# Reload of the node sums: the fourth tile's load moved behind the last tile's load

## The chip, the cores and the metric

The kernel runs on one core of a Trainium2 chip. The metric is the device time of one execution in microseconds (us), the median over several runs; lower is better. A core has a matrix engine (TensorE, "PE" in the profile), a vector engine (VectorE, "DVE"), a scalar engine (ScalarE, "ACT"), a general engine (GpSimd, "POOL") and an engine that issues most of the transfers (SyncE, "SP"). SP, ACT and POOL each have a DMA queue; in the profile SP's is q1, ACT's is q10 and POOL's is q0. All of them are served by the same 16 DMA engines. Engines wait for one another on semaphores.

## The reference, cut to what matters

A graph layer over 625 nodes with 512 features each and 10625 edges: a tensor-product message per edge, summed by target node; a linear-attention mixing of the nodes; and a feed-forward stage with two shared experts and 64 routed ones, of which each node takes six.

```python
xn = layernorm(x)
x1 = xn[src].reshape(-1, 16, 32); x2 = edge_attr.reshape(-1, 16, 32)
contrib = coeffs[None, :, None] * x1[:, i1, :] * x2[:, i2, :]      # 64 paths
edge_out = zeros.at[:, i3, :].add(contrib)
gnn = zeros.at[dst].add(edge_out)                                   # sum over edges by node
x = x + gnn + linear_attention(xn)
x = x + moe(layernorm(x))                                           # 2 shared, 64 routed, top 6
```

## The kernel before, in words

The edges are sorted by target node. The nodes are cut into ten windows of 64 (`NW = 10`, `W = 64`), numbered w = 0 to 9; the last window holds nodes 576 to 624. A window is worked in four chunks of 16 paths (`CHUNKS = 4`), so there are 40 chunks k. For a chunk DVE multiplies the gathered node rows with the edge rows (L1202, one instruction per path), and PE sums the products by target node with one-hot matrices (L1667; L1675 for the last window) into PSUM banks.

When a window's four chunks are summed, ACT copies the two banks to a staging buffer and stores them to `sums_d` in DRAM (`flush`, L870 to L874): two DMAs of 64 rows of 4 KB, 512 KB in all, each counted by `s_stored[w % 2]`. This is done for windows 0 to 8. The ninth window (w = 8) is the last one stored in this way, and the change speaks of it as the ninth group. The tenth window isn't stored: its sums are added from PSUM by DVE (`add_last`, L1296).

The sums come back in another tiling. The array `sums` has five tiles t = 0 to 4 of 125 nodes, with a row of 2048 numbers (8 KB) for each node, and lies in the SBUF tensor `arena`. Each tile is loaded by two DMAs, rows 0 to 111 and rows 112 to 124 (`PARTS`), except the last tile (nodes 500 to 624). Of that only the 76 rows of nodes 500 to 575 come from DRAM, by DMAs of 64 and 12 rows; the rest has been cleared by ACT (L879, `s_zeroed`). Tile 3 is nodes 375 to 499 and so needs windows up to w = 7 only (nodes 448 to 511); tile 4 needs the ninth window, w = 8 (nodes 512 to 575).

SP's program at this place (L522 to L532), in its order: wait until DVE has finished the products of window 8 (`s_prod`), wait until windows 0 to 7 are stored, load tiles 0 to 3 (eight DMAs, L528), wait until ACT has cleared the rest of tile 4, wait until window 8 is stored (`s_stored[0]`), load tile 4's rows (two DMAs, L532). Each of the ten DMAs adds 16 to `s_sums`. After them SP waits for the last chunk on PE (`s_chunk`) and then issues the loads of the feed-forward weights (L565, L554, L557, L568, L560), the first ones without a wait between them.

DVE, when it has made the last products, waits for all ten loads at once (`dve.wait_ge(s_sums, 16 * 10)`, in `sum_and_normalize`), adds the tenth window (L1296) and sums the 64 paths into the node features (`path_sum`, L1288); then come the layer norm (L1314 to L1330), the transposes on PE (L1764), the router and the experts. A branch for edges that the fixed windows don't hold (`missed`) isn't taken with these inputs.

Of the kernel before, what the change touches and what calls it, by code (L numbers as in the profile page):

```python
# [22 lines left out]
TT, TR, DC = 5, 125, 4  # L23
HALVES = ((0, 313), (313, 312))
PARTS = ((0, 112), (112, TR))
# [13 lines left out]
LATE = (NW - 1) * W - (TT - 1) * TR  # L39
TOP = 64  # L40
# [129 lines left out]
def gps_layer(nc, x, src, dst, edge, coeffs, paths, wqkv, rm, wout, bout,  # L170
              wr, swg, swu, swd, wg, wu, wd, out):
    with ExitStack() as ctx:
# [5 lines left out]
        def sem(name):  # L178
            return ctx.enter_context(nc.semaphore(name))
# [13 lines left out]
        prod, x1, x2, stage, sums, pair = m["prod"], m["x1"], m["x2"], m["stage"], m["sums"], m["pair"]  # L193
# [146 lines left out]
        s_sums = sem("s_sums")  # L340
# [8 lines left out]
        onehot, rtab, rank, selb, parts, cnt_row, extra = (m[k] for k in ("onehot", "rtab", "rank", "selb", "parts",  # L349
                                                                         "cnt_row", "extra"))  # L350
# [125 lines left out]
        def _(sp):  # L476
# [45 lines left out]
            sums_tiles = sums_d[0:N, :].rearrange("(t p) c -> p t c", t=TT)  # L522
            sp.wait_ge(s_prod, CHUNKS * (NW - 1))
            for b in range(2):
                sp.wait_ge(s_stored[b], 32 * (NW // 2 - 1))
            for t in range(TT - 1):
                for a, b in PARTS:
                    sp.dma_start(sums[a:b, t, :], sums_tiles[a:b, t, :]).then_inc(s_sums, 16)  # L528
            sp.wait_ge(s_zeroed, 1)
            sp.wait_ge(s_stored[0], 32 * (NW // 2))  # L530
            for a, b in ((0, TOP), (TOP, LATE)):
                sp.dma_start(sums[a:b, TT - 1, :], sums_tiles[a:b, TT - 1, :]).then_inc(s_sums, 16)  # L532

            sp.wait_ge(s_cover, 1)
            missed = sp.value_load(more_v[:, :], min_val=0, max_val=1)
# [1450 lines left out]
```

## Time and profile before

| | us |
|---|---|
| median of 3 runs | 1015.66 |
| lowest and highest run | 1013.46, 1018.88 |
| the profiled execution, its own time | 1019.58 |
| the profiled execution, span from first to last instruction | 1017.5 |
| PE busy | 895.9 (88% of the span) |
| DVE busy | 548.1 (54%) |
| ACT busy, POOL busy | 256.0 (25%), 268.2 (26%) |
| data moved by DMA | 300.68 MB, mean 296 GB/s |
| mean granted TensorE clock | 0.961 |

The span falls into an edge stage (to about 321 us), the sum over the paths with the layer norm and the router (to about 396 us), and the experts. Times in the profile are counted from the first instruction. A DMA that an engine issues shows as a short row at its issue; its packets run later on the DMA engines. The view of the DMA queues counts, for a stretch of time, each queue's packets that started in it, their megabytes, and the time that they took as a share of the time of 16 engines. A packet of a tile reload is a row of 8 KB, one of a store of window sums 4 KB. Each DMA engine that takes part in a DMA closes it with a packet of 4 bytes, the completion; it counts as "under 512 B". The view counts a DMA of 112 rows with its completions as 128 packets, one of 13 rows as 26.

### The profile page before, as it was taken

To read this page: it belongs to the slowest core of one execution; us is meant where nothing else is said; L and a number is where in the kernel's file an instruction comes from. 1 tells how busy PE (TensorE), PEld (TensorE's weight loads), DVE (VectorE), ACT (ScalarE), POOL (GpSimd) and SP (SyncE) were. 2 spreads that over 40 slices of the span, in tenths; PEclk is the share of its full clock that TensorE was granted. 3 is DMA by queue.
4 is the path that set the end of the run, shared out by engine and by line. 5 is a ranking of instruction groups with operands and counts; after the bars stand their busy time and mean duration, and the time that the engine had idled before them with its cause. 6 is when DMAs were issued, how large, how long until landed. Compare 5 with 4: busy or idle time off the path is not lost. (4 is left out here: it accounts for less than half of the span.)

```text
span 1017.5 us, 20833 instructions
## 1 busy us (share of the span) xinstructions
PE 895.9 (88%) x7497; PEld 589.3 (58%) x7497; DVE 548.1 (54%) x1623; ACT 256.0 (25%) x573; POOL 268.2 (26%) x265
## 2 busy tenths in 40 slices
PE   1599998897878298999999999999999989999991
PEld 1355555564544196676556566766676765656660
DVE  7997987978798986323324333334233332333216
ACT  2111101121130132333322322333233322322331
POOL 4543321334300102222222222222222322222211
PEclk9699999999989789999999999999999999999996
DMA  8856454565428951889979999999988999999976
GB/s 276 287 207 207 158 186 171 207 207 208 166 63 279 373 206 57 319 303 367 405 290 334 359 383 413 390 387 361 405 307 332 353 400 398 365 374 366 402 289 262
DMA packets 76929, 300.68 MB, mean 296 GB/s; under 512 B 13730, under 2 KB 14119, under 8 KB 58548
## 3 DMA queue, kind: packets, MB, share of 16 engines
q1 hardware_dynamic: 57256, 254.21, 65.9%
q0 software_dynamic: 17280, 38.48, 10.5%
q10 hardware_dynamic: 2252, 6.06, 1.7%
q8 instruction: 95, 1.56, 0.6%
q14 instruction: 46, 0.38, 0.1%
HBM read 290.26 MB, written 26.62 MB: 311 GB/s over the span
## 5 line engine op out<-in xcount | busy, mean ns | idle before, releaser
L1202 DVE TENSOR_TENSOR arena<-arena 128x288 f32 (+1 forms) x640 | 236.3, 449 | 37.8 <-remote 24.5
L1826 PE MATMUL bank<-arena,low 128*64 128x256 f32 x2048 | 241.6, 383 | 2.0 <-issue 2.0
L1667 PE MATMUL bank<-arena,multi 128*64 128x256 f32 x1296 | 162.0, 400 | 44.0 <-DVE arena L1202 32.6
L1826 PEld LDWEIGHTS bank<-arena,low 128*64 128x64 f32 x2048 | 141.0, 137 | 75.6 <-issue 12.4
L1851 PE MATMUL bank<-arena,low 128*64 128x256 f32 x1392 | 161.6, 379 | 1.1 <-ACT low L980 1.1
L1667 PEld LDWEIGHTS bank<-arena,multi 128*64 128x64 f32 x1296 | 99.5, 144 | 102.2 <-issue 44.2
L743 POOL DMA_INDIRECT low<-xr_d,idx x64 | 90.2, 1409 | 238.7 <-DVE place L1433 177.6
L747 POOL DMA_INDIRECT y_d<-low,place x64 | 68.5, 1070 | 262.3 <-ACT low L987 181.8
L1851 PEld LDWEIGHTS bank<-arena,low 128*64 128x64 f32 x1392 | 101.3, 137 | 50.3 <-ACT low L980 1.3
L987 ACT ACTIVATE low<-bank,gcol 64x256 f32<-64x256 f32 x174 | 82.1, 472 | 105.0 <-PE bank L1851 103.9
L687 POOL DMA_INDIRECT arena<-xn_d,ssel x79 | 90.3, 1143 | 38.2 <-issue 21.8
L1438 DVE TENSOR_TENSOR low<-low,bank 128x256 f32<-128x256 f32 x64 | 39.2, 613 | 103.4 <-ACT low L983 102.8
L1492 DVE TENSOR_TENSOR low<-low,bank 64x512 f32<-64x512 f32 x23 | 24.7, 1075 | 101.9 <-ACT low L1023 80.7
L1791 PE MATMUL bank<-xT_,arena 128*128 128x208 f32 (+1 forms) x384 | 74.8, 349 | 5.1 <-ACT low L970 2.6
L983 ACT ACTIVATE low<-bank 128x256 f32<-128x256 f32 x64 | 24.7, 386 | 207.1 <-PE bank L1826 207.1
L1791 PEld LDWEIGHTS bank<-xT_,arena 128*128 128x128 f32 x384 | 67.9, 192 | 11.9 <-issue 8.9
L1836 PE MATMUL bank<-arena,low 128*32 128x256 f32 x928 | 55.5, 381 | 0.2 <-issue 0.2
L1417 DVE TENSOR_TENSOR low<-iota,multi 125x640 bf16<-125x640 f32 x64 | 52.2, 816 | 0.0
L977 ACT COPY low<-bank 128x512 f32<-128x512 f32 x64 | 37.6, 587 | 37.8 <-PE bank L1815 35.5
L1836 PEld LDWEIGHTS bank<-arena,low 128*32 128x32 f32 x928 | 27.9, 110 | 25.5 <-issue 9.5
L1815 PE MATMUL bank<-ident,low 128*128 128x128 f32 x256 | 40.7, 281 | 2.2 <-DMA low<-xr_d,idx 1.7
L1815 PEld LDWEIGHTS bank<-ident,low 128*128 128x128 f32 x256 | 28.9, 140 | 22.0 <-issue 19.5
(214 smaller groups left out, 710.9 us busy)
## 6 DMA issues: line engine op xcount, KB each, us to landing
arena<-in_L_ffn_Wg_dram SPq DMA_DIRECT2D x64, 1024.0 KB
arena<-in_L_ffn_Wu_dram SPq DMA_DIRECT2D x64, 1024.0 KB
arena<-in_L_ffn_Wd_dram SPq DMA_DIRECT2D x64, 1024.0 KB
arena<-in_edge_attr_dram SPq DMA_DIRECT2D x88, 256.0 KB
arena<-y_d SPq DMA_DIRECT2D x5, 1250.0 KB, 6.8
sums_d<-arena ACTq DMA_DIRECT2D x18, 256.0 KB, 3.2
arena<-sums_d SPq DMA_DIRECT2D x4, 896.0 KB
arena<-in_L_mix_W_qkv_dram SPq DMA_DIRECT2D x2, 1024.0 KB, 18.1
```

The lines of the kernel that those rows point to most:

```text
L687: pool.indirect_dma_start(x1[b][:, i, :], None, xn_d, bass.IndirectOffsetOnAxis(ap=ssel[:, at + i:at + i + 1], axis=0)).then_inc(s_x1[b], 16)
L743: return pool.indirect_dma_start(xg[:, to, :], None, xr_d, bass.IndirectOffsetOnAxis(ap=idx[:, i:i + 1], axis=0), bounds_check=N - 1, oob_ ...
L747: return pool.indirect_dma_start(y_d, bass.IndirectOffsetOnAxis(ap=place[:, i:i + 1], axis=0), yy[:, b, :], None, bounds_check=Y_ROWS - 1, ...
L987: ins = act.activation(yy[64 * o:64 * o + 64, b, h * HF:(h + 1) * HF], out_bank[64 * h:64 * h + 64, 0:HF], ACT.Copy, scale=gcol[64 * h:64 ...
L1202: return dve.tensor_tensor(prod[:, buf, 0:n, EXT * p:EXT * p + EXT], x1[b][:, 0:n, bass.ds(i1, EXT)], x2[b][:, 0:n, bass.ds(i2, EXT)], ALU ...
L1417: return dve.tensor_tensor(onehot[0:TR, b], iota[0:TR, None, bass.ds(base, CAP2)].to_broadcast([TR, TT, CAP2]), ranks[:, :, None].to_broad ...
L1667: ins = pe.matmul(bank[2 * b + c // 2][64 * h:64 * h + 64, 256 * (c % 2):256 * (c % 2) + 256], pair[:, pairs, i, :], prod[:, buf, i, 256 * ...
L1791: ins = pe.matmul(shared_bank(u)[:, 256 * w:256 * w + nn], shgu[:, w, k, c * 128:(c + 1) * 128], xT[:, k, a:a + nn], start=(w == 0 and k = ...
L1815: ins = pe.transpose(bank[1][:, c * 128:(c + 1) * 128], xg[:, b, c * 128:(c + 1) * 128], ident[:, :])
L1826: ins = pe.matmul(out_bank[64 * h:64 * h + 64, w * HF:(w + 1) * HF], xgT[:, b, k, 64 * o:64 * o + 64], gu[:, slot, w, k, h * HF:(h + 1) * HF],
L1836: ins = pe.matmul(out_bank[at:at + PART, q * HF:(q + 1) * HF], xgT[:, b, k, CAP + PART * q:CAP + PART * (q + 1)], gu[:, slot, w, k, h * HF ...
L1851: ins = pe.matmul(out_bank[64 * h:64 * h + 64, 0:HF], lhs, dn[:, slot, k, h * HF:(h + 1) * HF], start=(k == 0), stop=(k == DC - 1), skip_g ...
```

## The change

SP loads only tiles 0, 1 and 2 at once. The two waits (on the clearing and on the store of window 8) come next, then the load of tile 4's rows, and after it the load of tile 3. No transfer is added or dropped, the sizes are the same, and DVE still waits for all ten. The loop has become a helper `reload`, so all of these DMAs are recorded under L528; lines below the place have four added to their number.

```diff
-            for t in range(TT - 1):
-                for a, b in PARTS:
+            def reload(t, parts):
+                for a, b in parts:
                     sp.dma_start(sums[a:b, t, :], sums_tiles[a:b, t, :]).then_inc(s_sums, 16)
+
+            reload(0, PARTS)
+            reload(1, PARTS)
+            reload(2, PARTS)
             sp.wait_ge(s_zeroed, 1)
             sp.wait_ge(s_stored[0], 32 * (NW // 2))
-            for a, b in ((0, TOP), (TOP, LATE)):
-                sp.dma_start(sums[a:b, TT - 1, :], sums_tiles[a:b, TT - 1, :]).then_inc(s_sums, 16)
+            reload(TT - 1, ((0, TOP), (TOP, LATE)))
+            reload(3, PARTS)
```

SP's row before, from the last edge load to the next wait; the 112- and 13-row loads are tiles 0 to 3, the 64- and 12-row loads tile 4:

```order
L495 DMA arena<-in_edge_attr_dram 128x512
L528 DMA arena<-sums_d 112x2048 [waits s_stored1,s_stored0,s_prod]
L528 DMA arena<-sums_d 13x2048
L528 DMA arena<-sums_d 112x2048
L528 DMA arena<-sums_d 13x2048
L528 DMA arena<-sums_d 112x2048
L528 DMA arena<-sums_d 13x2048
L528 DMA arena<-sums_d 112x2048
L528 DMA arena<-sums_d 13x2048
L532 DMA arena<-sums_d 64x2048 [waits s_stored0,s_zeroed]
L532 DMA arena<-sums_d 12x2048
L535 TENSOR_LOAD more_v [waits s_cover]
```

The same piece of SP's row in the changed kernel:

```order
L495 DMA arena<-in_edge_attr_dram 128x512
L528 DMA arena<-sums_d 112x2048 [waits s_stored1,s_stored0,s_prod]
L528 DMA arena<-sums_d 13x2048
L528 DMA arena<-sums_d 112x2048
L528 DMA arena<-sums_d 13x2048
L528 DMA arena<-sums_d 112x2048
L528 DMA arena<-sums_d 13x2048
L528 DMA arena<-sums_d 64x2048 [waits s_stored0,s_zeroed]
L528 DMA arena<-sums_d 12x2048
L528 DMA arena<-sums_d 112x2048
L528 DMA arena<-sums_d 13x2048
L539 TENSOR_LOAD more_v [waits s_cover]
```

The fourth pair of 112 and 13 rows has moved past the wait and past the 64 and 12 rows; six loads stand ahead of the wait in place of eight. No other engine's row changes, apart from line numbers.

## Rows read from the trace of the kernel before

**Rows 1.** Waits on PE, from 358 us to the end: total, times, longest.
```profile
PE bank L1791 <- ACT low L970: 2.6, 1, 2.6
```
**Rows 2.** Busy time in stretches: PE, PEld, DVE, ACT, POOL, clock, DMA share, GB/s.
```profile
357.60:361.50 3.90, 3.86 (x17) 3.16 (x18) 3.87 (x6) 1.81 (x4) 0.00 (x0) 0.50 1.01 426
361.50:366.20 4.70, 4.70 (x44) 4.70 (x44) 3.87 (x4) 2.38 (x3) 0.00 (x0) 0.99 1.01 360
...
396.00:1012.00 616.00, 592.37 (x5485) 388.06 (x5485) 214.79 (x703) 181.47 (x406) 155.47 (x126) 0.99 0.92 354
```
**Rows 3.** Waits of SP's queue, 290 to 325 us.
```profile
SPq L528 <- DVE arena L1202: 17.4, 1, 17.4
SPq L530 <- DMA sums_d<-arena: 14.1, 1, 14.1
```
**Rows 4.** Timeline, 285 to 375 us: start, duration, what, idle before it.
```profile
297.49 3.57 SPq L528 DMA_DIRECT2D arena<-sums_d  x8
...
300.40 17.20 DVE L1202 TENSOR_TENSOR arena<-arena 128x224 f32 x56
...
302.77 1.10 ACTq L874 DMA_DIRECT2D sums_d<-arena  x2
...
315.22 1.07 SPq L532 DMA_DIRECT2D arena<-sums_d  x2
...
321.33 0.85 DVE L1296 TENSOR_TENSOR arena<-arena,bank 61x256 f32<-61x256 f32 x2 [3.73 <-DMA arena<-sums_d]
...
324.45 6.87 SPq L560 DMA_DIRECT2D arena<-in_L_ffn_Wd_dram  x2
...
357.64 4.42 PE L1764 MATMUL bank<-ident,low 125*128 125x125 f32 x20 [19.38 <-DVE low L1330]
```
**Rows 5.** DMA queues, 297.4 to 302.7 us: packets, MB, share of 16 engines.
```profile
q1 hardware_dynamic: 151, 1.07, 80.2%
```
**Rows 6.** DMA queues, 302.7 to 308.9 us, the stretch behind the store's issue.
```profile
DMA packets 194, 1.30 MB, mean 210 GB/s; under 512 B 35, under 2 KB 35, under 8 KB 35
q1 hardware_dynamic: 194, 1.30, 97.3%
```
**Rows 7.** DMA queues, 308.9 to 311.1 us.
```profile
q1 hardware_dynamic: 67, 0.52, 61.0%
q10 hardware_dynamic: 66, 0.26, 37.3%
```
**Rows 8.** DMA queues, 311.1 to 312.1 us.
```profile
q10 hardware_dynamic: 45, 0.13, 64.2%
q1 hardware_dynamic: 37, 0.17, 49.0%
```
**Rows 9.** DMA queues, 312.1 to 314.3 us.
```profile
q1 hardware_dynamic: 80, 0.56, 76.4%
q10 hardware_dynamic: 49, 0.13, 23.9%
```
**Rows 10.** DMA queues, 314.3 to 316.3 us; no packet of q10.
```profile
q1 hardware_dynamic: 72, 0.43, 85.4%
```
**Rows 11.** DMA queues, 316.3 to 321 us.
```profile
DMA packets 120, 0.67 MB, mean 143 GB/s; under 512 B 38, under 2 KB 38, under 8 KB 38
q1 hardware_dynamic: 119, 0.66, 62.4%
```
**Rows 12.** Timeline, ACT, 60 to 300 us: two other stores of window sums.
```profile
186.64 1.10 ACTq L874 DMA_DIRECT2D sums_d<-arena  x2
...
276.39 1.10 ACTq L874 DMA_DIRECT2D sums_d<-arena  x2
```
**Rows 13.** DMA queues, 277.45 to 279.75 us; no packet of q10 from 276.39 to 277.45.
```profile
q10 hardware_dynamic: 160, 0.52, 84.9%
```
**Rows 14.** DMA queues, 186.64 to 189.3 us; q10's 160 packets follow by 191.6.
```profile
q0 software_dynamic: 212, 0.70, 69.4%
q1 hardware_dynamic: 192, 0.33, 34.1%
```

## The prediction

> **What bounds the kernel now.** I read the whole from the end. Behind 358 us PE hardly waits: its longest wait after the router begins is 2.6 us [rows 1], and over the 616 us of the experts it is busy 592.37 us [rows 2]. What arrives late at the start of that stretch therefore comes late at the end, nearly one for one. The start is set by DVE: PE sat idle 19.38 us before L1764, until DVE had finished the layer norm [rows 4], and DVE works without a gap worth naming from L1296 at 321.33 us. What released L1296 is the place of the change: DVE made its last product by 317.60 us (300.40 + 17.20) and idled 3.73 us for the loads from `sums_d` [rows 4]. So these loads are on the path that sets the end, and 3.73 us is also the most that any order of them could bring, 0.37% of the time.
>
> Next, what makes the loads late. SP's own waits [rows 3]: 14.1 us for the store of the ninth group, before tile 4's load. That looks like the thing to shorten. But the DMA view of the same stretch shows that the wait costs little: q1 carries the reloads all along. Its packets up to 321 us are 151, 194, 67, 37, 80, 72 and 119 [rows 5 to 11], together 720. Four tiles make 4 x (128 + 26) = 616, tile 4's part (64 rows with 16 completions, 12 with 12) makes 104: 720 again, so nothing is missing from the count. By 316.3 us 601 had started, 15 short of tile 3's end; tile 4's load was issued at 315.22 and needs about one more microsecond to its first packet. Tile 4 joined the end of tile 3 almost without a hole. The loads are bound by the pace of their queue, not by the wait.
>
> **What the change does to the sum.** It removes and adds nothing: the same ten loads, 4.72 MB, on the same queue, the same wait on DVE. It takes 154 of the 720 packets (tile 3, 1.02 MB) out of the part that is queued before the wait and puts them behind it. So the question is whether q1 still has work while SP waits.
>
> 1. Tiles 0 to 2 are 3 x 154 = 462 packets. By 312.1 us 449 of q1's packets had started (151 + 194 + 67 + 37, [rows 5 to 8]). In the new kernel q1 runs dry soon after 312.1.
>
> 2. When does the store land? It was issued at 302.77 [rows 4]; up to 308.9 there is no packet of q10 at all [rows 6]; then the two queues take turns, 66 against 67 packets [rows 7]. By 312.1, 111 of its 160 packets had started; the other 49 took until 314.3 beside tile 3 [rows 8, 9]. Nothing in the first 6 us changes if the cause is the load already in progress, so I keep the start at 308.9. Only the last 49 packets lose their competitor. Alone, 160 packets took 2.3 us [rows 13], so 49 would take 0.7 and end at 312.8; if the slowest engine is still busy with tile 2 they end as before, 314.3. I take 313.4.
>
> 3. From the landing to SP's issue: 314.3 to 315.22 is 0.9 us. From an issue to the first packet in a quiet stretch: 276.39 to 277.45, 1.05 us [rows 12, 13]. First packet of tile 4 at 313.4 + 0.9 + 1.05 = 315.35. Between some 312.5 and 315.35 q1 moves nothing, where before it moved tile 3.
>
> 4. Then 201 rows, 1.65 MB. Before, the last 271 packets of q1, likewise 1.65 MB, ran from 312.1 to 321, 8.9 us with the tail of the slowest engine [rows 9 to 11]. At the pace of a full queue, 210 GB/s [rows 6], they would take 7.8 us. I take 8.4: last packet at 323.75, and DVE starts 0.3 us later, as before (321.0 to 321.33): 324.05.
>
> The wait ends 2.7 us later than 321.33. The bounds: landing at 312.8 and tile 0's pace (1.07 MB in 5.3 us less the first 1.05 [rows 5], 252 GB/s, so 6.5 us) give 321.55, +0.2 us. Landing at 314.3, tile 4 at 210 GB/s (3.0 us) and tile 3 at the 143 GB/s of the last stretch [rows 11] (7.2 us) give 326.75, +5.4 us.
>
> **What is queued behind the longer wait.** On SP, after the two moved loads, come the wait for the last chunk and the weight loads. They were issued from 320.94, behind a wait for PE; the moved loads are issued by about 316.4, so SP isn't late, but the first weights now stand behind tile 3 on the same queue. PE starts again only at 357.64 [rows 4], and with transposes that need no weights, so that lateness of a few us is covered by more than 30. ACT and PE wait for nothing that moves. PE's idle time before L1764 grows from 19.38 to about 22 us. After that gap the granted clock is 0.50 up to 361.5 and 0.99 behind it [rows 2], the 1.2 and the 2.4 GHz level; a later start can shift that edge as well. I cost it at nothing in the forecast and at half of a 3.9 us stretch, 2 us, in the slow rival.
>
> Against its own profiled execution the sum is 1019.58 + 2.7 = 1022.3. The profiled execution is 3.9 us above the median of the runs, so the forecast for a median is 1015.66 + 2.7 = 1018.4.
>
> **A rule of the skill beside it.** Rows 6 and 7 show 6.1 us without a packet of the store and equal turns behind it. The Trainium skill, page "DMA: Bandwidth & Descriptors", section "Queues, rings and completion order", says that each DMA engine goes round between the queues that have work, a packet at a time. By the rule alone the store would take its turns from about 303.8 in both kernels, and the rule doesn't explain the 6.1 us. Where the store shared the engines the trace agrees with it; where it stood still, it does not. If the start of the store came from the queue ahead of it, it could move with the change, and that is the first rival.
>
> **Rivals.** *The store starts earlier.* With six loads ahead of it in place of eight, it might begin one tile sooner: at 308.9 two tiles were through (345 packets had started, two tiles are 308, [rows 5, 6]); should the chip let a store in when only two queued tiles are left, that point is one tile sooner now. If it begins near 304.5 and takes the 5.4 us that it took beside the loads, it lands at 309.9, SP issues at 310.8, the first packet comes at 311.85, before q1 is dry. Then there is no hole, the same 720 packets run at the same pace, and the wait ends as before: 0 us, 1015.7. For it: a store issued at 276.39, with no work on q1, started after 1.05 us, and one at 186.64, with 192 packets of q1 ahead, only after 2.7 [rows 12 to 14]; work on q1 does hold a store back. Against it: SP could put seven larger loads and more into the queue before it was held, at 324.45 for 6.87 us [rows 4], so eight reloads are not beyond what the queue takes, and the store passed tiles 2 and 3, so it didn't wait for all that was issued before it.
>
> *The mixture is faster.* Beside the store q1 moved 0.52 MB in 2.2 us, 236 GB/s, against 210 alone [rows 6, 7]. If the store starts early and the whole queue holds that pace, 4.72 MB take 20.0 us from 298.5, and DVE starts at 318.8: 2.5 us sooner, 1013.2. Against it: in the other shared stretch q1 moved only 0.17 MB in 1.0 us [rows 8].
>
> *Slower.* The store lands no sooner than before and tile 3, now last, meets the slow end of the queue, where 0.67 MB took 4.7 us [rows 11]: the upper bound above, +5.4 us, 1021.1; with the clock's edge moved as well, up to 1023. This decides if the store's last packets are held by the slowest engine's tile 2 and not by tile 3.
>
> **How the numbers follow.** Forecast (+2.7 us, 0 to +4): 0.50. The store starts earlier (0 us): 0.25. Faster mixture (-2.5 us): 0.08. Slower (+5.4 to +7.4 us): 0.17. Half a percent is 5.1 us, about what a measurement of this kernel tells from no change (its three runs lie 5.4 us apart). Faster by more than that is beyond the 3.73 us that DVE idles, so it needs the spread of the runs: 0.04. Slower by more: most of the slow rival and a little of the forecast's spread: 0.12. Within: 0.84. The range takes in the faster mixture in part and the upper bound, with some 1.5 us for the spread of a median: 1013.2 to 1022.5.
>
> **What would show it.** In the new profile: SP's wait for the store shorter by about 1 us and not by 4 or 5; a stretch of 2 to 3 us around 313 to 315 us in which q1 moves nothing; tile 4's issue near 314.3; weight loads still issued at 321; DVE idle before L1300 (L1296 before) about 6.4 us in place of 3.73; everything behind it later by the same amount. The prediction is wrong if the store's first packet comes before 307, if q1 has no hole, or if DVE's idle time stays near 3.7 us.

## The result, and the profile after

The changed kernel takes 1020.64 us (median of 20 runs), the kernel before 1016.73 us (20 runs). The ratio of their runs is 1.0043, with a 95% interval of 1.0027 to 1.0059: slower by 4.4 us, between 2.7 and 6.0 (the two medians are 3.9 us apart). The forecast was +2.7 us, at the lower edge of that interval; 1020.64 lies in the forecast's range, 1013.2 to 1022.5.

The profiled execution of the changed kernel spans 1020.0 us against 1017.5. Its first reload is issued 4.1 us earlier than before (293.40 against 297.49), which is the spread of the edge stage, so I compare stretches and not points of time. The timeline of the changed kernel, same columns as [rows 4]; the ten loads are now one merged row because they share a line:

```profile
293.40 18.94 SPq L528 DMA_DIRECT2D arena<-sums_d  x10
...
298.69 1.10 ACTq L878 DMA_DIRECT2D sums_d<-arena  x2
...
316.97 0.37 SPq L569 DMA_DIRECT2D arena<-in_L_ffn_sWg_dram  x1
...
321.01 0.85 DVE L1300 TENSOR_TENSOR arena<-arena,bank 61x256 f32<-61x256 f32 x2 [7.37 <-DMA arena<-sums_d]
...
357.45 4.30 PE L1768 MATMUL bank<-ident,low 125*128 125x125 f32 x20 [23.16 <-DVE low L1334]
```

DVE now idles 7.37 us for the loads in place of 3.73 [rows 4], 3.64 us more. From the first reload's issue to DVE's add it is 27.61 us against 23.84, from that add to PE's transposes 36.44 against 36.31. PE's idle time in front of the transposes grew by 3.78 us. The 3.7 us arise at the reload, and the stage from the add to the transposes passes them on whole. How much of them reaches the end only the runs tell: in single profiles the time from the transposes to the end of the span scatters more than that, 659.9 us before, 662.6 in the changed kernel, and 657.6 in e4 below.

SP's wait for the store, changed kernel, against 14.1 us in [rows 3]:

```profile
SPq L534 <- DMA sums_d<-arena: 14.3, 1, 14.3
```

It begins about 1 us earlier, since two issues fewer stand ahead of it, and ends hardly sooner. The DMA queues of the changed kernel, in this order: 298.65 to 304.9 us; 304.9 to 307.1; 307.1 to 308.1; 308.1 to 309.9; 309.9 to 311.5; 311.5 to 315.9; 315.9 to 320.1.

```profile
DMA packets 188, 1.25 MB, mean 201 GB/s; under 512 B 35, under 2 KB 35, under 8 KB 35
...
q1 hardware_dynamic: 65, 0.52, 62.7%
q10 hardware_dynamic: 63, 0.26, 36.5%
...
q1 hardware_dynamic: 38, 0.20, 53.8%
q10 hardware_dynamic: 52, 0.14, 53.4%
...
q10 hardware_dynamic: 45, 0.12, 31.4%
q1 hardware_dynamic: 18, 0.02, 5.5%
...
DMA packets 0, 0.00 MB, mean 0 GB/s; under 512 B 0, under 2 KB 0, under 8 KB 0
...
q1 hardware_dynamic: 138, 0.90, 99.1%
...
q1 hardware_dynamic: 155, 1.03, 98.9%
```

The first three stretches repeat [rows 6 to 8] almost packet for packet: again no packet of the store for 6.3 us after its issue, then equal turns. Then comes what before was tile 3 beside the end of the store [rows 9, 10]: q1 moves 0.02 MB in 1.8 us, and for 1.6 us nothing moves at all. q1 is short of work from 308.1 to 311.5, 3.4 us; between 309.49 and 311.73, 2.2 us, it starts no packet at all. By then 462 packets have started, three tiles. The reload's other 258 run from 311.73 to 319.99 us. The last two stretches hold 293 packets of q1, and the 35 beyond the 258 are rows of the weight loads, which SP issues from 316.97 us on.

### The profile page after: what moved, and what is told of

Its sections match the earlier page's. It is cut to its first block, busy times and chain, and to the rows that moved or that the text cites. A ratio compares the mean times of both kernels' runs of the same rounds, so it can differ in the third digit from the quotient of the medians.

```text
span 1020.0 us, 20833 instructions
## 1 busy us (share of the span) xinstructions
PE 896.4 (88%) x7497; PEld 587.8 (58%) x7497; DVE 548.4 (54%) x1623; ACT 255.3 (25%) x573; POOL 267.3 (26%) x265
## 4 chain that ended last, share of the span: by engine, by line
PE 70%; DVE 13%; issue 5%; DMA 4%; DVEq 4%; another core or an unknown queue 1%; ACT 1%; ACTq 0%; SPq 0%; POOL 0%; POOLq 0%
PE bank L1830 23%; PE bank L1855 15%; PE bank L1671 7%; DVE arena L1206 7%; PE bank L1795 5%; PE bank L1840 5%; PE bank L1807 4%; PE bank L1819 3%; DVEq L1204 2%; PE bank L1606 2%; PE bank L1824 2%; DMA sums_d<-arena 1%; DVEq L1221 1%; PE bank L1848 1%
```

## The experiments

In each single profile I read two numbers: the time from the first reload's issue to DVE's add (before 23.84, changed 27.61) and DVE's idle time in front of it. Each kernel was profiled once; the two with the reload of before, before and e8, differ by 0.13 and 0.08 us in them. Ratios are to the kernel before, on the same chip, with 95% intervals.

| kernel | reload to add, us | DVE idle, us | ratio |
|---|---|---|---|
| before | 23.84 | 3.73 | 1 |
| changed | 27.61 | 7.37 | 1.0043 (1.0027 to 1.0059) |
| e1 no wait, other rows | 23.79 | 3.77 | 1.0033 (1.0009 to 1.0058) |
| e8 control for e1 | 23.71 | 3.65 | 1.0047 (1.0029 to 1.0064) |
| e2 tile 3 behind the wait, tile 4 last | 27.19 | 7.07 | 1.0040 (1.0015 to 1.0065) |
| e3 two tiles behind | 26.41 | 5.85 | 1.0042 (1.0013 to 1.0072) |
| e4 only 13 rows behind | 23.53 | 3.53 | 1.0013 (0.9992 to 1.0035) |
| e5 paced | 26.58 | 5.01 | 1.0029 (1.0008 to 1.0050) |
| e6 128-row loads, order of before | 21.88 | 1.86 | 1.0009 (0.9988 to 1.0030) |
| e10 e6 again, other chip | 22.46 | 1.85 | 1.0000 (0.9980 to 1.0019) |
| e7 128-row loads, changed order | 22.79 | 2.25 | 1.0002 (0.9981 to 1.0023) |
| e9 e6 with early register loads | 21.85 | 0.05 | 0.9987 (0.9971 to 1.0004) |

### e1 and e8: the order without the wait

```diff
             reload(1, PARTS)
             reload(2, PARTS)
-            sp.wait_ge(s_zeroed, 1)
+            sp.wait_ge(s_zeroed, 2)
+            for a, b in ((0, TOP), (TOP, LATE)):
+                sp.dma_start(sums[a:b, TT - 1, :], sums_tiles[a:b, 0, :]).then_inc(s_sums, 16)
+            reload(3, PARTS)
             sp.wait_ge(s_stored[0], 32 * (NW // 2))
-            reload(TT - 1, ((0, TOP), (TOP, LATE)))
-            reload(3, PARTS)
```

`s_zeroed` is waited for at 2 in place of 1, so SP waits for all of ACT's clearing; it cost nothing that shows, the ten loads of e1 were issued in one go, in 5.1 us.

> The order of the changed kernel (tiles 0, 1, 2, tile 4's 76 rows, tile 3), but the 76 rows are read from the start of sums_d (nodes 0 to 75) and not from the ninth group's, so their load needn't wait for its store; part of the last tile's sums is therefore not the reference's. Theory H (the loss is the stretch in which q1 is empty while SP waits): no hole, DVE idles 3.3 to 4.3 us before the last window's add, as before, and the time is that of before within 1 us. Rival O (the loss comes from the order: the large tile with its slow last packets stands at the end): the loss stays, idle 6.5 us or more, time 3 to 4 us over before.

DVE's wait, on one row of the timeline of e1:

```profile
318.24 0.85 DVE L1301 TENSOR_TENSOR arena<-arena,bank 61x256 f32<-61x256 f32 x2 [3.77 <-DMA arena<-sums_d]
```

The idle time is that of before although tile 3 stands last. So tile 3 at the end of the queue costs nothing here, and theory H holds for DVE's wait. But the time didn't come back: the ratio is 1.0033. That was against my expectation and needed a control, since e1's features differ. e8 keeps the order and the waits of before and changes only the source rows:

```diff
-                sp.dma_start(sums[a:b, TT - 1, :], sums_tiles[a:b, TT - 1, :]).then_inc(s_sums, 16)
+                sp.dma_start(sums[a:b, TT - 1, :], sums_tiles[a:b, 0, :]).then_inc(s_sums, 16)
```

> The control for e1: order and waits of before, but tile 4's 76 rows are read from nodes 0 to 75, so the features of those nodes, and with them the choice of experts, are e1's and not the reference's. If e1's 0.33% came from its data (its PE ran 7549 matmuls, 52 more than before), this kernel is slower by the same 0.2 to 0.4%, runs 7549 matmuls, and DVE idles 3.7 us as before. If it came from e1's order, this kernel takes the time of before, ratio 0.999 to 1.001.

The profile page's row of busy time, share and instructions by engine, of e8:

```profile
PE 889.6 (89%) x7549; PEld 585.9 (59%) x7549; DVE 548.7 (55%) x1625; ACT 256.5 (26%) x576; POOL 279.6 (28%) x265
```

Both run the same 7549 matmuls, where every other kernel here, with the reference's data, runs 7497, and e8 is slower by 0.47% with an unchanged reload, which is what was expected if the cause was the data. The data, through the choice of experts, account for e1's excess; its reload is as fast as before. With the data alone 1.0047 and with data and order 1.0033, the order adds nothing; the changed kernel's loss on top of e8's would have given about 1.009. (On the chip of e8, e9 and e10 the kernel before took 998.18 us; each ratio is within one chip.)

### e2: the same order as before, but behind the wait

```diff
-            reload(TT - 1, ((0, TOP), (TOP, LATE)))
             reload(3, PARTS)
+            reload(TT - 1, ((0, TOP), (TOP, LATE)))
```

> Tiles 0, 1, 2, the wait for the store, then tile 3 and at the end tile 4's 76 rows: the order of before, with tile 3 behind the wait. Theory H: the same hole of 1.5 to 3 us as in the changed kernel, DVE idle 7 to 8 us, time 3 to 5 us over before. Rival O: the order is that of before, so idle 3.7 us and no loss.

DMA queues of e2, 308.5 to 310.5 us; then its row of DVE:

```profile
DMA packets 4, 0.01 MB, mean 4 GB/s; under 512 B 2, under 2 KB 2, under 8 KB 4
```

```profile
319.76 0.86 DVE L1300 TENSOR_TENSOR arena<-arena,bank 61x256 f32<-61x256 f32 x2 [7.07 <-DMA arena<-sums_d]
```

Here tile 3 precedes tile 4 as it did before, and the loss is there in full, with 2.0 us in which 4 packets start. Rival O, that the order makes the loss, falls. Together with e1 this is the pair that decides: order of the change without the hole, no loss at the reload; order of before with the hole, the loss.

### e3: two tiles behind the wait

```diff
             reload(1, PARTS)
-            reload(2, PARTS)
             sp.wait_ge(s_zeroed, 1)
             sp.wait_ge(s_stored[0], 32 * (NW // 2))
             reload(TT - 1, ((0, TOP), (TOP, LATE)))
+            reload(2, PARTS)
             reload(3, PARTS)
```

> Only tiles 0 and 1 are queued ahead of the wait; then tile 4's rows, tile 2, tile 3. Theory H with the store's start set by what q1 has in progress when it is issued (and not by how many loads are queued): first packet of the store again 6 to 6.5 us after its issue, the store then runs alone and lands about 8.7 us after its issue; q1 is empty for some 4 us; DVE idle 8 to 9 us, 4 to 5 us over before. Rival N (the store is held back by the number of loads queued ahead): with four ahead it starts 1 to 3 us after its issue, lands within 7 us, q1 never runs empty, idle 3.7 us, no loss.

DMA queues of e3, 303.05 to 306.15 us, from the store's first packet on:

```profile
q10 hardware_dynamic: 160, 0.52, 50.7%
```

Neither expectation was right in its numbers. The store began 3.4 us after its issue, in place of 6.2, and all of its 160 packets started within 3.1 us, so it landed 6.5 us after its issue, as N had it. It didn't keep the old start, as I had expected of H, and q1 did run empty, for 3.05 us (from 10.45 to 13.5 us behind the first reload's issue), as N had not. The add came 2.6 us later than before; I had expected 4 to 5. The ratio, 1.0042, is too wide to say more. So the start of the store does depend on what is ahead of it, once that is little.

### e4: only the small part behind

```diff
+            reload(3, PARTS[:1])
             sp.wait_ge(s_zeroed, 1)
             sp.wait_ge(s_stored[0], 32 * (NW // 2))
             reload(TT - 1, ((0, TOP), (TOP, LATE)))
-            reload(3, PARTS)
+            reload(3, PARTS[1:])
```

> Only tile 3's 13-row part (26 packets, 0.11 MB) is behind tile 4's rows; its 112-row part (0.92 MB) is queued ahead of the wait as before. Theory H: the 112 rows carry q1 over the wait, DVE idle 3.5 to 4.5 us, time as before within 1 us. Rival O: the 13-row part, which uses few engines, comes last, 1 to 2 us lost.

DVE's add on the timeline of e4:

```profile
320.20 0.85 DVE L1301 TENSOR_TENSOR arena<-arena,bank 61x256 f32<-61x256 f32 x2 [3.53 <-DMA arena<-sums_d]
```

With the 112 rows ahead of the wait the loss at the reload is gone, and rival O's 1 to 2 us don't come. They carry q1 across the wait only just: from 313.8 to 315 us q1 starts 6 packets, in the last 1.2 us before tile 4's rows. So a short thin stretch costs nothing that shows. The amount queued ahead of the wait is what counts.

### e5: pacing SP

```diff
             reload(0, PARTS)
+            sp.wait_ge(s_flush, NW - 1)
             reload(1, PARTS)
             reload(2, PARTS)
```

> The order of the changed kernel, but behind tile 0's two loads SP waits until ACT has copied the ninth group out of PSUM, that is until just before ACT issues the store; then tiles 1 and 2, the wait for the store, tile 4's rows, tile 3. If the store is held only by packets of q1 already under way: its first packet comes 1 to 3 us after its issue, it lands by 7 us after it, tile 4's load is issued while tiles 1 and 2 still run, no hole; DVE idle 3.3 to 4.5 us, time as before within 1 us, the changed kernel's loss gone. If the store is slow for another cause (its start 6 us after issue again): hole and loss as in the changed kernel, idle 7 us or more.

DMA queues of e5, 300.6 to 302.3 us:

```profile
DMA packets 0, 0.00 MB, mean 0 GB/s; under 512 B 0, under 2 KB 0, under 8 KB 0
```

This failed as a repair. SP's new wait left q1 without work for 1.7 us ahead of tile 1, one hole in place of another, and the store still began only 4.5 us after its issue, although q1 had nothing in progress when it was issued: tiles 1 and 2 were issued within 1.2 us of it and came first. Neither of the two expectations, a start after 1 to 3 us or again after 6, was met. DVE idles 5.01 us in place of the 3.3 to 4.5 expected of the repair.

### e6, e10 and e7: the shape of the loads

```diff
-            reload(0, PARTS)
...
+            sp.dma_start(arena_t[:, 0, :], sums_d[TR * 0:TR * 0 + 128, :]).then_inc(s_sums, 16)
...
-                dve.wait_ge(s_sums, 16 * 10)
+                dve.wait_ge(s_sums, 16 * 6)
```

Tiles 1 to 3 likewise, from row 125 t on (`TR` is 125); `arena_t` is `sums` with all 128 partitions. There are six loads in place of ten. e6 and e10 keep the order of before, e7 has that of the change.

> The order of before (tiles 0 to 3 ahead of the wait, tile 4 behind it), but tiles 0 to 3 are loaded by one DMA of 128 rows each, the last three rows into partitions that nobody reads, in place of 112 + 13 rows. Theory P (the pace of the reload, 210 GB/s, comes from the shape of its DMAs over the 16 engines; the weight loads of 128 rows of 8 KB run at over 400 GB/s): a packet takes about 0.31 us in place of 0.5, tiles 0 to 3 end some 5 us sooner, the store lands sooner too, DVE idle 0 to 1.5 us, time 2 to 3.7 us under before. Rival M (the pace comes from sums_d in DRAM, not from the shape): packets still 0.5 us, idle 3.3 to 4 us, time as before.

> e6 once more, beside e9 on one chip. In e6 the add came 1.96 us sooner after the first reload's issue than before, but the ratio was 1.0009 (0.9988 to 1.0030). If the earlier add counts in full, the ratio is 0.998; if something behind it gives the gain back, it is again 1.000 or over, and the profile shows a longer time from the add to the end of the experts than the 696 us of before.

> The same 128-row DMAs in the changed kernel's order (tiles 0, 1, 2, wait, tile 4's rows, tile 3). Theory P: q1 is through with three tiles about 9 us after the first issue, so it runs empty all the longer, but what remains behind the wait takes about 5 us less: DVE idle 1 to 4 us and still 1.5 to 3 us longer than with 128 rows in the order of before. Rival M: as the changed kernel, idle 7 us, 3 to 4 us over before.

DMA queues of e6, 293 to 301.35 us, from the first reload's packets to the store's first:

```profile
DMA packets 413, 3.10 MB, mean 372 GB/s; under 512 B 35, under 2 KB 35, under 8 KB 35
```

The pace is 372 GB/s against the 210 of [rows 6]: theory P holds, the shape of the DMAs set the pace and not `sums_d`. DVE no longer waits for a DMA. Its row in the waits of e6:

```profile
DVE arena L1303 <- issue: 1.9, 1, 1.9
```

The 1.9 us that remain are DVE's own, more than the 0 to 1.5 us expected.

In the changed order (e7) DVE waits for the loads again, 2.25 us, and the add comes 0.9 us later than in e6, not the 3.8 us that separate the same two orders with slow loads, and less than the 1.5 to 3 us that I expected.

The time did not follow. The ratios are 1.0009 (e6), 1.0000 (e10) and 1.0002 (e7), where the 1.96 us of e6, counted in full, would be 0.998. e6's interval leaves 0.998 out, e10's just holds it. From the add to the end of the span it is 697.3 us in e6 and 697.1 in e10, 1.2 and 0.9 us more than the 696.2 of before, as the second of e10's two expectations had it. Part of that is visible. PE in e6, from its first transpose, with the columns of [rows 2]:

```profile
350.39:356.40 6.01, 5.98 (x28) 5.28 (x28) 5.97 (x8) 3.49 (x6) 0.00 (x0) 0.50 0.99 406
```

The granted clock stays at 0.50 for about 6 us of PE's work in place of 3.9 [rows 2], and the work up to L1791 (L1798 in e6) takes 9.5 us against 8.6 before; in e10 it was 9.45. That is half of the gain in these two profiles. It doesn't follow from the earlier start alone, as the last section shows, and whether the gain reaches the end of the kernel in the median stays open.

### e9: DVE's last 1.86 us

```diff
                 if c == 3 and 1 <= w < NW - 1:
                     dve.wait_ge(s_turn, 2 * w)
+                if k == HOT - 1:
+                    dve.load(more_offs, toff[0:1, 32:48])
+                    missed = dve.value_load(more_v[:, :], min_val=0, max_val=1)
```

> 128-row loads in the order of before (e6), and DVE's register loads and its read of the branch flag, which e6 left as the last 1.86 us between the last product and the add, moved ahead of the last chunk's products. If those 1.86 us are these loads: idle 0.5 to 1.2 us, time 0.6 to 1.3 us under e6. If they are the branch itself (fetching instructions behind it), idle stays at 1.8 us and the time at e6's. Against before both give a ratio of 0.996 to 0.998 if an earlier add counts in full at the end.

DVE's timeline in e9:

```profile
292.55 4.92 DVE L1209 TENSOR_TENSOR arena<-arena 128x224 f32 x16 [1.80 <-issue]
297.53 0.85 DVE L1306 TENSOR_TENSOR arena<-arena,bank 61x256 f32<-61x256 f32 x2
```

The idle time in front of the add is gone, and 1.80 us stand in front of the last chunk instead. So the 1.86 us were the register loads and the read of the flag, not the branch. They cost their time wherever they stand and only moved: the reload to the add is 21.85 us, e6's 21.88. I had expected 0.5 to 1.2 us of idle time there and hadn't counted the loads at their new place. e9's median is 0.8 us under e10's on the same chip, inside the 0.6 to 1.3 expected, but the two intervals overlap and the profile shows no earlier add, so this isn't evidence of a gain. The ratio, 0.9987 (0.9971 to 1.0004), is the lowest of all, and it does not clear 1.

## Why the prediction was right

The mechanism held step by step, and e1, e2 and e4 show it against the rival of the order. q1 ran dry where step 1 put it; the store's start didn't move (6.3 us behind its issue, 6.2 before); a hole of 2.2 us in q1 followed, forecast at 2 to 3; DVE's add and PE's start came later. The sizes:

| step | forecast | measured |
|---|---|---|
| store, first packet behind its issue | 6.2 us | 6.3 us |
| store, last packet behind its issue | 10.6 us (0.9 sooner) | 11.1 us (0.4 sooner) |
| last packet to SP's issue, issue to first packet | 0.9 + 1.05 us | 0.6 + 1.3 us |
| 201 rows | 8.4 us | 8.3 us |
| last packet to DVE's add | 0.3 us | 1.0 us (0.5 before) |
| DVE's idle time | 6.4 us | 7.37 us |
| time | +2.7 us (0 to +4) | +4.4 us (2.7 to 6.0) |

Two terms were too small. The store's last 49 packets were to win 0.9 us when tile 3 no longer competed; they won 0.4. The trace doesn't show what held them. The last 45 started over 1.8 us, and q1, with 18 packets of tile 2, the last at 309.49 us, took only 5.5% of the engines' time in it; step 2 had named a slowest engine still busy with tile 2 as the case in which nothing is won. And I took the 0.3 us between the last packet and DVE from the edge of a window. The last packet before started at 320.82 us, so it was 0.5 us even there; in the changed kernel it was 1.0. Together, 0.5 and 0.7 us, less 0.2 us by which two other terms were too large, they are the 1 us by which DVE's idle time was under-forecast. The 0.7 us between DVE's 3.7 and the 4.4 of the runs lies within the interval. The 4.4 us stands a little above the 0 to +4 of the forecast's own line. That the whole range, 9.3 us wide, held the result says little; what speaks for the mechanism are the profile and the experiments.

One of the signs failed. SP's wait for the store was to be about 1 us shorter; it was 14.3 us in place of 14.1. The forecast had the store land 0.9 us sooner, and left out that with two issues fewer the wait also begins 0.9 us sooner. The mechanism doesn't rest on it. Two other signs came as told: tile 4's issue 17.1 us behind the first reload's, which is 314.5 us on the scale of before, and the first weight load 23.6 us behind it, 23.5 before.

The claim that 3.73 us was the most that any order could bring was an overstatement. With the loads entirely out of the way DVE still idles 1.86 us (e6; 1.85 in e10) for its own register loads, so the most was 1.9 us, and the runs of e6 and e10 don't even show that.

The rival in which the store starts earlier was wrong for this change, and e3 shows where it would be right: with two tiles ahead the store does start 2.8 us sooner behind its issue. It doesn't help, because q1 is then dry all the same. The rival of the faster mixture failed: 65 packets of q1 in 2.2 us beside the store, 67 before. The slow rival's last tile at 143 GB/s did not occur: the 201 rows, 1.65 MB, took 8.3 us, 199 GB/s. In the last 4.2 us q1 moved 1.03 MB, 0.29 MB of it the first rows of the weights; before, nothing followed on the queue there.

## What to carry to other kernels

A long wait of an issuing queue costs nothing while the queue has transfers in front of it. Before moving a transfer behind a wait, count the packets that stay ahead and see whether they outlast the wait: here 462 packets did not outlast a store that landed 16.4 us behind the first load's issue; 616 did, and 590 (e4) nearly. If a reload itself is on the path, look at its shape before its order. And when an experiment changes data that choose later work, run the control with the data alone.

## What the runs showed of the hardware that was not expected

**A store can stand behind many packets of another queue.** From 1.1 us behind the store's issue (the time a store takes to start on a quiet chip) to its first packet, q1 started this many packets:

| kernel | loads issued and not done | packets of q1 | us |
|---|---|---|---|
| before | tiles 0 to 3 | 165 | 5.05 |
| changed | tiles 0 to 2 | 166 | 5.15 |
| e6 | four tiles of 128 rows | 147 | 2.85 |
| e7 | three tiles of 128 rows | 138 | 3.10 |
| e5 | tiles 1 and 2 | 96 | 3.40 |
| e3 | tiles 0 and 1 | 84 | 2.30 |

The row for the changed kernel, 299.8 to 304.95 us:

```profile
q1 hardware_dynamic: 166, 1.11, 100.1%
```

With much queued ahead it is nine to ten packets for each of the 16 engines, whether a packet takes 0.5 us or 0.3, and whether six loads are queued or eight; with less queued it is less. Counted from the store's issue itself the first four rows are 192, 189, 203 and 198, some twelve for each engine. It is no fixed number for all transfers: behind the store issued at 64.44 us in the kernel before, beside edge loads with rows of 2 KB and POOL's gathers, q1 started 396 packets, 25 for each engine, in 4.2 us before the store's first.

The Trainium skill ("DMA: Bandwidth & Descriptors", section "Queues, rings and completion order") says that an engine going round between queues drains a whole packet of one before it switches, typically about 9 to 17 descriptors and at most 64. A packet of the profile here is one row, so if a row is one descriptor, the twelve of each engine lie in the page's typical span, and the 25 beside the edge loads above it but under its ceiling. The prediction had read the page's packet as one row, and so found nothing in the rule for the 6.1 us. Behind the delay the trace doesn't agree with turns of that length: 63 packets of the store and 65 of q1 start in 2.2 us, about four of each for an engine. No run here tests the rule by itself, and what holds the store until its first packet stays open.

**The shape of a load sets its pace.** Tiles of 112 + 13 rows of 8 KB ran at 210 GB/s, single DMAs of 128 rows of the same size from the same tensor at 372. The Trainium skill (same page, section "Rules for kernel authors") asks for 128 partitions and at least 1 MiB in a DMA for maximum bandwidth, and this agrees with it. It is also the one edit here that brought DVE's add forward by more than the scatter. Whether the 112 rows or the extra small DMA cost the pace was not separated.

**The clock's step behind an idle gap fell at different times, and did not follow PE's start.** In every profile the granted clock fell to 0.50 in PE's gap before the transposes and rose to 1.00 some time after PE had begun again. The part of the low stretch in which PE works lasted 3.9 us before [rows 2] and 3.6 in the changed kernel, where PE started later; 5.9 in e6 and 5.8 in e10, where it started sooner; but 3.5 in e7 and 3.1 in e9, where it started sooner as well, and 4.6 in e4 and 4.9 in e8, where DVE's add came as before. The rows of the changed kernel and of e9 (columns as in [rows 2]; the first one reaches past the step):

```profile
357.45:361.30 3.85, 3.85 (x18) 3.15 (x19) 3.81 (x6) 1.82 (x4) 0.00 (x0) 0.54 1.03 436
...
333.97:337.02 3.05, 3.05 (x14) 2.64 (x15) 3.02 (x5) 1.25 (x3) 0.00 (x0) 0.50 1.03 427
```

The clock also fell again later, for 3.4 us of PE's work at a time: between 362 and 990 us once in the profile before (385.5 to 388.9 us), twice in the changed kernel's (384.9 to 388.3 and 398.6 to 402.0), and not at all in e4's. PE is busy through these stretches, so each costs up to 1.7 us, half of its length, by my estimate. An edit worth 2 us or less is therefore hidden in a single profile's span, and only the ratio over many runs can show it. That the change's loss, 3.7 us at the reload, came through is shown by its ratio; that e6's gain was taken back by the clock is not.
